# Expert tiles of the second half of a sparse MoE stage taken two at a time instead of one at a time

## The reference

```python
probs = jax.nn.softmax(router_logits.astype(jnp.float32), axis=-1)
topk_w, topk_idx = lax.top_k(probs, K)
topk_w = topk_w / jnp.sum(topk_w, axis=-1, keepdims=True)
...
hdn = jax.nn.silu(x @ gw) * (x @ uw)
return (acc + c[:, None] * (hdn @ dw), None)
...
out = expert_out + jax.nn.sigmoid(x @ shared_expert_gate_w) * shared_out
```

## Time and profile before

| | us |
|---|---|
| three runs | 1058.29, 1063.65, 1048.96 |
| median | 1058.29 |
| span of the profiled execution | 1061.5 |
| of it: tiles 0 to 63 in pairs (688 to 757) | 69 |
| of it: tiles 64 to 183 one at a time (757 to 1005) | 248 |
| of it: what follows (1005 to 1061.5) | 56.5 |

### The profile page before, as it was taken

One profiled execution on the slowest core, in us unless ns is written; L12 is line 12 of the kernel. 1 busy time (PEld: TensorE's weight loads), 2 busy tenths in 40 slices (PEclk: granted clock), 3 DMA queues, 4 the chain that ended last, 5 costly groups with the idle time before them and its releaser, 6 DMA issues.

```text
span 1061.5 us, 20791 instructions
## 1 busy us (share of the span) xinstructions
PE 883.7 (83%) x6317; PEld 686.6 (65%) x6317; DVE 643.0 (61%) x1912; ACT 539.8 (51%) x1294; POOL 563.7 (53%) x752
## 2 busy tenths in 40 slices
PE   5988999999999996887688751899976868587788
PEld 4767777777777774665465431598875757467645
DVE  6766777778877867776666543534434334244575
ACT  2425766767667755554444434366653334344412
POOL 3686675765768620046465547339835443432361
PEclk9978999999999999887878775599989777878899
DMA  5201122122221136686344272277756555565441
GB/s 145 64 13 43 50 74 79 51 80 76 80 71 46 41 73 170 210 247 217 122 156 130 78 248 101 93 245 228 219 184 194 176 177 180 177 182 163 150 153 45
DMA packets 125897, 138.80 MB, mean 131 GB/s; under 512 B 25174, under 2 KB 111766, under 8 KB 125790
## 3 DMA queue, kind: packets, MB, share of 16 engines
q1 hardware_dynamic: 114270, 106.01, 33.5%
q0 software_dynamic: 11520, 31.47, 9.5%
HBM read 76.44 MB, written 60.83 MB: 129 GB/s over the span
## 4 chain that ended last, share of the span: by engine, by line
PE 66%; DVE 15%; issue 8%; another core or an unknown queue 5%; ACT 2%; DMA 2%; SPq 2%; POOL 1%; DVEq 0%; ACTq 0%
PE bank L2415 7%; PE bank L2429 6%; PE bank L774 3%; PE bank L2374 3%; PE bank L776 3%; PE bank L726 3%; DVE xmax L1537 3%; PE bank L1527 2%; PE bank L803 2%; PE bank L2395 2%; PE bank L2406 2%; PE bank L2203 2%; PE bank L1604 2%; PE bank L433 2%
## 5 line engine op out<-in xcount | busy, mean ns | idle before, releaser
L2648 POOL DMA_INDIRECT got_rows<-ys,slot_idx x120 | 116.6, 972 | 158.2 <-DMA ys<-y_tile 62.7
L1852 POOL DMA_INDIRECT xs<-xrow,slot_idx x120 | 115.5, 962 | 87.7 <-DVE slot_idx L1939 35.2
L964 ACT ACTIVATE probs<-bank 128x512 f32<-128x512 f32 x192 | 113.9, 604 | 85.7 <-PE bank L776 48.6
L2415 PE MATMUL bank<-up_res,x_turned 128*128 x480 | 90.4, 319 | 60.9 <-ACT x_turned L2500 32.3
L1704 ACT ACTIVATE probs<-bank 128x512 f32<-128x512 f32 x128 | 74.4, 597 | 104.1 <-PE bank L1604 43.7
L2415 PEld LDWEIGHTS bank<-up_res,x_turned 128*128 128x128 f32 x480 | 75.7, 225 | 69.5 <-issue 69.3
L2558 DVE TENSOR_TENSOR hid_s<-gate_s,bank 128x128 f32<-128x128 f32 x120 | 34.4, 287 | 140.5 <-ACT gate_s L2505 100.6
L1537 DVE TENSOR_REDUCE xmax<-bank 128x2 f32<-128x512 f32 x128 | 86.0, 684 | 54.3 <-PE bank L1527 29.7
L1604 PE MATMUL bank<-query_x,keys_x 114*128 114x512 f32 x128 | 69.6, 549 | 16.7 <-DMA query_x<-xshift 7.9
L774 PE MATMUL bank<-query,keys 128*128 128x256 f32 x256 | 82.7, 347 | 0.5 <-ACT probs L964 0.4
L2429 PE MATMUL bank<-down_res,hid_t 128*128 x240 | 82.8, 432 | 0.1
(11 more groups left out here) (411 smaller groups left out, 2479.8 us busy)
## 6 DMA issues: line engine op xcount, KB each, us to landing
ys<-y_tile SPq DMA_DIRECT2D x62, 256.0 KB
xs<-zero_b SPq DMA_DIRECT2D x16, 512.0 KB, 3.2
up_res<-in_w_up SPq DMA_DIRECT2D x6, 1280.0 KB
ys<-xn SPq DMA_DIRECT2D x30, 256.0 KB
keys_x<-key_rows_x SPq DMA_DIRECT2D x32, 192.0 KB
ctx_in<-in_ctx SPq DMA_DIRECT2D x32, 128.0 KB, 2.5
key_rows_x<-ctx_hi SPq DMA_DIRECT2D x256, 16.0 KB, 1.5
query_x<-xq_rows_hi SPq DMA_DIRECT2D x64, 64.0 KB
```

The lines of the kernel that those rows point to most:

```text
L964: nc.scalar.activation(probs[:, u, :], SCORE[u % 2][:], ACT.Exp, scale=SCALE)\
L1852: nc.gpsimd.indirect_dma_start(out=xs, out_offset=bass.IndirectOffsetOnAxis(ap=slot_idx[:, r, k:k + 1], axis=0), in_=xrow[r % XROW_RING][: ...
L2415: last = nc.tensor.matmul(bank[2 + j % 2][:, 0:128], x_turned[j % 2][:, c * 128:c * 128 + 128], w[:, 256 * c:256 * c + 128], start=c == 0, ...
L2648: nc.gpsimd.indirect_dma_start(out=got_rows[:, g % GOT_RING, :], out_offset=None, in_=ys[0:T * (E + 8 * r + 8), :], in_offset=bass.Indirec ...
```

## The change

Tiles 64 to 183 become 60 pairs (pair numbers 32 to 91, `FIRST` = 32 to `TILE_PAIRS` = 92) and use the pair functions. Every step handles two tiles: `keep_pair` and `pair_out` copy 512 columns where `keep` and `rows_out` copied 256, `gate_pair` takes 128 where `gate` took 64, and each DVE step makes one instruction of 256 columns. The number of PE's matrix instructions stays. Distances that were counted in tiles are now counted in pairs: in step p PE does `turn_pair(p)`, `up_pair(p - 1)`, `turn_hidden(p - 3)`, `down_pair(p - 5)`, and ACT does `keep_pair(p)`, `gate_pair(p - 1)`, `pair_out(p - 5)`. Buffers for the larger pieces are taken from tiles that are free by then (`xrow`, `owner`). SP's program, POOL's program and the places of the combines are not touched.

```diff
+        pair_hid = [[hid_pairs[:, n, r, :] for r in range(2)] for n in range(2)]
+        gate_s = [owner[:, 4 + n, :] for n in range(2)]
+        hid_s = [xrow_all[:, 2, :], xrow_all[:, 3, :], xrow_all[:, 0, :]]
+        hid_t = [owner[:, 6:8, :], hid_pairs[:, 0], hid_pairs[:, 2]]
+        TURN_BANK, UP_BANK, DOWN_BANK = bank[0:2], bank[2:4], bank[6:8]
+        HID_BANK = [bank[4 + n][:, 0:256] for n in range(2)]
+        FIRST, TILE_PAIRS = E // 2, TILES // 2
...
+            for p in range(TILE_PAIRS + 5):
+                if p < TILE_PAIRS:
+                    values(p)
+                    turn_pair(p)
+                if 0 <= p - 1 < TILE_PAIRS:
                     up_pair(p - 1)
-                if p >= 2:
+                if FIRST <= p - 3 < TILE_PAIRS:
+                    turn_hidden(p - 3)
+                if 0 <= p - 2 < FIRST:
                     down_pair(p - 2)
-            for j in range(E, TILES + 5):
...
+                if FIRST <= p - 5:
+                    down_pair(p - 5)
...
-            for j in range(E, TILES + 6):
-                if E <= j - 6 < TILES:
-                    rows_out(j - 6)
-                if j < TILES:
-                    keep(j)
...
+                if FIRST <= p - 5:
+                    pair_out(p - 5)
...
-            for j in range(1, TILES + 3):
...
+            for j in range(1, TILES + 4):
+                if j % 2 == 1:
+                    if j < TILES:
+                        hidden_pair(j // 2)
+                    if FIRST <= j // 2 - 2 < TILE_PAIRS:
+                        hidden_turned(j // 2 - 2)
```

More of the change, by code:

```diff
@@ L1353, in build @@
         xnorm = sb("xnorm", [128, D])
-        xrow = [sb(f"xrow{n}", [128, D]) for n in range(XROW_RING)]
+        xrow_all = sb("xrow", [128, XROW_RING, D])
+        xrow = [xrow_all[:, n, :] for n in range(XROW_RING)]
         xden = sb("xden", [128, 2, XH])
@@ L2368, in values @@
                             at[k + a] = vals[a]
[L2370 to L2376, removed]
             def turn_pair(p):
@@ L2392, in up_pair, with turn_hidden @@
                 for r in range(2):
+                    out = UP_BANK[p % 2][:, 128 * r:128 * r + 128]
                     for c in range(2):
[L2394 to L2397 removed]
+                        x = pair_x[p % 2][:, r, c * 128:c * 128 + 128]
+                        if p < FIRST:
+                            at = 512 * first_pair(p) + 256 * c + 128 * r
+                            last = nc.tensor.matmul(out, up_res[:, at:at + 128], x, start=c == 0, stop=c == 1)
+                        else:
+                            w = up_res[:, ds(up_at[2 * p + r - E], 384)]
+                            last = nc.tensor.matmul(out, x, w[:, 256 * c:256 * c + 128], start=c == 0, stop=c == 1)
+                last.then_inc(S("tile_up"), 2)
+            def turn_hidden(p):
+                pe.wait_ge(S("tile_hidden"), ended("tile_hidden") + 2 * p + 2)
+                if p < FIRST + 2:
+                    pe.wait_ge(S("shared_added"), ended("shared_added") + 6)
+                else:
+                    pe.wait_ge(S("tile_hidT"), ended("tile_hidT") + 2 * (p - FIRST) - 2)
+                for r in range(2):
+                    last = nc.tensor.transpose(HID_BANK[p % 2][:, 128 * r:128 * r + 128],
+                                               hid_s[p % 3][:, 128 * r:128 * r + 128], ident[:])
+                last.then_inc(S("tile_hid_turned"), 2)
             def down_pair(p):
@@ L2405, in down_pair @@
                 for r in range(2):
-                    last = nc.tensor.matmul(bank[6 + p % 2][:, D * r:D * r + D], pair_hid[p % 2][r],
-                                            down_res[:, D * first_pair(p):D * first_pair(p) + D], start=True, stop=True)
-                last.then_inc(S("tile_down"), 2)
[L2410 to L2430, removed]
+                    out = DOWN_BANK[p % 2][:, D * r:D * r + D]
+                    if p < FIRST:
+                        last = nc.tensor.matmul(out, pair_hid[p % 2][r],
+                                                down_res[:, D * first_pair(p):D * first_pair(p) + D], start=True, stop=True)
+                    else:
+                        last = nc.tensor.matmul(out, hid_t[p % 3][:, r, :], down_res[:, ds(down_at[2 * p + r - E], D)],
+                                                start=True, stop=True)
+                last.then_inc(S("tile_down"), 2)
             odd_spread(pe)
@@ L2541, in hidden_pair @@
                 dve.wait_ge(S("tile_gated"), ended("tile_gated") + 2 * p + 2)
-                if p >= 2:
-                    dve.wait_ge(S("tile_down"), ended("tile_down") + 2 * p - 2)
-                for r in range(2):
-                    last = nc.vector.tensor_tensor(pair_hid[p % 2][r][64 * r:64 * r + 64, :],
-                                                   pair_gate[p % 2][:, 128 * r:128 * r + 128],
-                                                   bank[2 + p % 2][64:128, 128 * r:128 * r + 128], ALU.mult)
```

132 lines of the change are left out of this document (47 added, 85 removed).

## The result

| us, median (lowest to highest) | before | changed | ratio, 95% interval |
|---|---|---|---|
| first chip | 1059.01 (1048.96 to 1063.65) | 1069.18 (1063.38 to 1080.8) | 1.016 (1.008 to 1.023) |

The forecast was 1052. The change made the kernel 10 us slower, not 6 faster.

What follows compares the result with a forecast made beforehand. PE bounded the stage between gathers, ACT's handshakes during them; paired, the loop through SP would. Stage 228 us against 248, 20 gained less 14 for clock: net 6 off 1058.3, 1052 us. Own range 1038 to 1062, to 1066 with ACT's upper delay.

Steps and rivals of the forecast that it cites:

- The loop through SP: Result, store, load, landing in the paired stage: one step of slack, 6.6 to 6.7 us a round, 3.35 a pair.
- During the gathers: While POOL gathers, the round through SP grows to 9.35 us, 4.7 a pair; 25 pairs pass in 116.3 us.
- ACT's own delay before the copy: During gathers ACT starts the result copy 0.7 to 1.4 us late; 0.9 went into the round.
- ACT's delay goes by instruction: During gathers ACT's delay attaches to the instruction, not its size; a 4.4 us cycle of three now serves two tiles.
- the rival of delays by size: Instructions of 512 columns held twice as long during gathers: 13 pairs there, stage 268 us, 20 slower, 1078; chance 0.09.
- the 14 us for the clock: Half clock around eleven groups of gathers in the stage: 23 us if it fell as before; 14 of them taken.
- The stage sum: Paired stage: 14 first steps, 116.3 gathers, 94 for 28 steps, 4 at the end: 228 us against 248, before clock.
- The clock: PE's clock in the stage should fall less often, above 0.83, with PE busy 51% during gathers instead of 28%.
- The rival of a clock that stays low: PE idling 0.9 in every 3.35 us holds half clock: stage 294 us, 46 slower, 1104, or about 1080 partly; chance 0.15.
- The rule of the Trainium skill: Read as: a PE waiting for a load each step would oscillate in clock, giving the low-clock rival's time in part.
- The load not the bound: SP's chain is shorter than reckoned; halved handshakes leave a 198 us stage, gain 23 to 50, near 1023; chance 0.18.

Runs made afterwards that it cites:

- second trace: Unaltered changed kernel, profiled again in a later run because the first profile was slow: 1058.94 us, where the kernel before took 1060.7.
- the later stores: Changed kernel with SP storing pair p - 8, not p - 6, behind load p from pair 32: 929.46 and 930.38 us; elsewhere 1013.86 (0.955 of the kernel before).
- chip A: Kind of chip on which the kernel before takes 1048 to 1061 us; the first chip and two later ones.
- chips B: Kind of chip on which the kernel before takes 928 to 930 us; three chips.
- first trace: First profile of the kernel meant: changed kernel 1080.8 us (rounds, stage of 263); kernel before 1061.5 us (single tiles).
- the earlier trace: Profile of the kernel before, unchanged, from which the prediction was made: 1061.5 us.
- the copy's: Trace of an unchanged copy of the kernel before, run beside the changed kernels: 1058.93 us, 0.998 of the kernel before.
- the counters by one: Counters raised by one a pair, not two: on the changed kernel 1.079 and 1.082 of the kernel before; with later stores 0.952, 0.946 and 1.003.
- single tiles with later stores: Kernel before with SP storing pair p - 8 instead of p - 6 behind load p: 952.05 us, 1.027 of the kernel before.

## Why the prediction was wrong

**The loop through SP: right, and it is the cause.** Forecast one step of slack, 6.65 us a round and 3.35 a pair; measured 6.9 in the round shown and 3.5 over 42 pairs (3.2 in the second trace). What it costs is shown by the later stores: 52 to 60 us on a chip A, 71 and 76 on chips B. One reading in it was off without effect on the sum: from the end of the issues (912.37 and 0.85) to 914.8 are 1.6 us, not 1.8.

**During the gathers: the step that failed.** The prediction put a round at "6.65 + 1.0 + 0.8 + 0.9 = 9.35, so 4.7 us a pair", and counted 25 pairs in 116.3 us. By the gates there were 18, 6.5 us each. Seven pairs fewer, each made up at 3.35 outside, are 23 us; that alone turns 1052 into 1075. This count hangs on the edges of the stretches, though: `up_pair` starts 23 times on PE in the same twelve. The rounds themselves are safer. Followed one by one, from the start of `pair_out(q)` to that of `pair_out(q + 2)`, the 26 rounds of the first trace that lie more than half within gathers last 10.6 us in mean:

| mean of the rounds mostly within gathers, us | rounds | whole round | copy starts behind the end of `down_pair` | all the rest |
|---|---|---|---|---|
| forecast | | 9.35 | 0.9 | 8.45 |
| first trace (chip A) | 26 | 10.6 | 2.2, up to 7.0 | 8.4 |
| second trace (chip A) | 26 | 10.3 | 1.9, up to 6.9 | 8.4 |
| changed kernel on two chips B | 31, 32 | 8.3, 8.6 | 0.08 | 8.2, 8.5 |

So the mis-sized term is ACT's own delay before the copy: 0.9 in the sum, 2.2 in the run. A round serves two pairs, so in the first trace it makes 26 x 1.3 / 2 = 17 us of the 21 by which the stage exceeds its forecast of 242; in the second it is 13, where the stage exceeds it by 9. All the rest of the round was sized right in sum, and on chips B, where ACT is not held, nothing is left of the term. The 0.9 came from "one to two of the smallest gaps"; the idle times ahead of the two copies in the earlier trace rows are 2.13 and 2.60. The timeline of ACT and SP in a group of gathers shows such a hold:

```profile
899.70 0.59 ACT L2462 COPY x_turned_more<-bank 128x512 f32<-128x512 f32 x1 [1.91 <-PE bank L2374]
905.42 0.28 ACT L2474 ACTIVATE owner<-bank 128x128 f32<-128x128 f32 x1 [5.14 <-PE bank L2391]
905.60 0.58 ACT L2481 COPY xn<-bank 128x512 f32<-128x512 f32 x1
...
899.59 1.44 SPq L2297 DMA_DIRECT2D ctx_in<-xs  x2
906.20 0.38 SPq L2302 DMA_DIRECT2D ys<-xn  x1
906.81 0.87 SPq L2297 DMA_DIRECT2D ctx_hi<-xs  x2
```

and PE beside them:

```profile
898.18 1.06 PE L2391 MATMUL bank<-up_res,x_turned 128*128 x8
...
899.29 1.03 PE L2420 MATMUL bank<-down_res,hid_pairs 128*128 x4
902.39 0.66 PE L2374 MATMUL bank<-ident,ctx_in 128*128 128x128 f32 x4 [2.06 <-issue]
902.88 1.06 PE L2391 MATMUL bank<-up_res,x_turned_more 128*128 x8
...
910.20 1.12 PE L2374 MATMUL bank<-ident,ctx_hi 128*128 128x128 f32 x4 [5.17 <-DMA ctx_hi<-xs]
```

The result that `pair_out` copies at 905.60 had been ready since 900.32 (899.29 and 1.03). The gate ahead of it in ACT's order, at 905.42, belongs to the `up_pair` of 898.18 (ACT does `keep_pair(p)`, then `gate_pair(p - 1)`), which had ended at 899.24; of the two runs of L2391 above it is the earlier. So both had their inputs, and ACT ran nothing from 900.29 to 905.42; the group's last gather ended at 903.76. Why ACT is held no run tells. The loop hands the hold on: the store goes at 906.20, the load at 906.81, and PE has its data at 910.20. Then PE, after standing still for more than 5 us, wakes at a lower clock, 0.50, the lower level of 1.2 GHz:

```profile
911.00:914.00 3.00, 3.00 (x14) 2.91 (x13) 0.53 (x2) 0.86 (x2) 2.30 (x3) 0.50 0.18 52
```

**ACT's delay goes by instruction: right, as far as the counts tell.** With the loop open, a pair takes 4.1 us during the gathers, as a single tile took 4.2 in the first trace and 3.6 in the copy's (by counted gates; the 4.4 of the prediction went by their busy time). With the edges of the stretches moved to the gathers themselves it is 4.0 a pair and 3.1 a tile. What needs no edges: an instruction of ACT whose inputs were ready and whose engine was free started 0.6 us late in mean during gathers in three traces of single tiles and 0.7 in two of pairs with later stores, at up to twice the columns. So the rival of delays by size, which doubled them, falls (its 1078 also left out the 14 us for the clock, with which it would be 1092). It is from this that the pairs can gain: 4.5% with the later stores, 4.8 and 5.4% with the counters by one as well, on chips A. That it is the pairs' gain and not the later stores' rests on the kernel before, whose PE never waits for a load, and is not shown by a run: single tiles with later stores were timed only on a chip B, where they lose.

**The stage sum.** 228 us and 14 for the clock were forecast; 263 and 251 were measured. Outside the gathers 42 pairs took 146 and 136 us, where the sum had 35 in 112 (28 steps in 94, the first seven in 14, and 4 for the last pairs' way) and 14 for the clock.

**The clock: right in direction.** It rose to 0.88 and 0.89, and half clock took 61 and 55 us of the stage instead of 85. In three rounds of the first trace that are clear of gathers PE's step lasts 5.0 us at half clock instead of 2.6, and the whole round 9.2 to 9.3 instead of 6.6 to 6.9. The rival of a clock that stays low, 1104 us, did not come: with the loop binding, PE idles in nearly every step, and this stretch of the changed kernel on a chip B, in which PE waited 1.76 us for a load ahead of 800.71, is at full clock (2.4 GHz) throughout:

```profile
797.00:803.00 6.00, 4.24 (x32) 3.68 (x31) 1.44 (x4) 2.31 (x5) 4.05 (x5) 1.00 0.80 238
```

The rule of the Trainium skill that was set beside this rival ("TensorE: Matmul & The Clock Gate", section "HAM oscillation — how this bites in real kernels") describes throttling in each tile behind a wait for its transfer, in a loop whose work is shorter than that wait. The prediction read more into it: by its own figures a step has 2.42 us of work and 0.9 of wait, so the rule did not speak for this rival. At waits of this length the traces do not show it; behind the waits of 5 us in a group of gathers they do.

**The load not the bound: wrong as a rival, but near to the repaired kernel.** It gave 23 to 50 us if the loop did not bind; the later stores, which open it, gained 47 us over the kernel before on a chip A (1060.7 to 1013.9), and 58 with the counters by one, above that range.

**What no step had: the chip.** The loss of the changed kernel is 1.6% and 0.4% (the latter not clear of zero) on chips A and 8% on chips B. On a chip B ACT is not held up during gathers, single tiles run at PE's pace all through, and there are no delays to halve: the loop's cost, 73 to 76 us, stands alone. On a chip A the gain of pairs during the gathers pays most of it back.

## What to carry to other kernels

When steps are made larger and their distances kept in number, count again every loop that leaves the engines: here a store behind a result and a load behind that store kept their places, and seven small steps of slack became one large one. Shift the far end of the loop together with the steps, and check the buffers on its other side (pairs had room for the later stores, single tiles did not). And when a disturbance holds up an engine of such a loop, size its term by the mean delay ahead of the very instruction in the loop, not by the smallest gap in a timeline: here it was 2.2 us and not 0.9.

The best version, later stores with counters by one, takes 0.946 and 0.952 of the kernel before on chips A and 1.003 (1.000 to 1.006) on a chip B.

## What the runs showed of the hardware

The same program takes 928 to 930 us on three chips and 1048 to 1061 on three others. The instructions themselves last the same (ACT's 256-column copy 0.372 and 0.373 us, POOL's gather 0.97 on both kinds). The stage of single tiles, from its first gate to its last, takes 243.0 us in the first trace and 146.3 on a chip B, 97 of the 134 by which the spans differ: on chips A the starts on ACT during gathers come late (4.2 and 3.6 us a tile), on the chip B traced they do not (1.23), while the DMA engines are busy 0.89 to 0.95 of the time and move 274 to 294 GB/s there against 0.54 to 0.74 and 165 to 226 in the twelve stretches of the first trace, of which the earlier trace rows shows two. What differs between the chips no run here tells.
